# Two neighbouring blocks' outputs in one buffer and one 1 MB store, the last two blocks stored singly

## The chip, the cores and the metric

The kernel runs on one core of a Trainium2 chip. A core has a matrix engine (TensorE, PE), a vector engine (VectorE, DVE), a scalar engine (ScalarE, ACT), GpSimd (POOL) and a sync engine (SyncE, SP), which work side by side and wait for each other by semaphores; data move between the chip's memory (DRAM) and the on-chip buffers by DMA, on 16 DMA engines. The metric is the device time of one execution in microseconds; lower is better.

## The reference

The input is four images of 256 channels by 64 by 64 pixels in f32. Layer 0 normalises each image in 32 groups and adds a 3 by 3 neighbourhood attention to the input. Layer 1 takes the pixels as tokens, adds a gated windowed mean over 64 tokens, and then a mixture of eight experts of which each token uses two. Cut to the part that the changed stage completes:

```python
def _from_tokens(t, like):
    B_, C_, H_, W_ = like.shape
    return t.transpose(0, 2, 1).reshape(B_, C_, H_, W_)

x = x + _L0_conv_ref(_gn(x), ...)
t = _to_tokens(x)
t = t + _L1_attn_ref(_ln_t(t), ...)
t = t + _L1_ffn_ref(_ln_t(t), ...)     # out = tokens + combine[:, e:e+1] * y for each expert e
x = _from_tokens(t, x)
```

## The kernel before

The kernel handles the image in NB = 32 blocks of BT = 512 pixels (eight rows of 64), eight blocks (IB) to an image. It has three loops, one after the other. The token loop makes the tokens and scatters each to its two experts. The expert loop runs 71 tiles of 512 tokens through the experts' two layers and scatters the answers, two for each token, into the DRAM tensor `answers`. The output loop, which this case is about, takes for each block the two answers of each of its 512 tokens, adds them, turns them from tokens to channels, and stores them to `out_x`.

The output loop is laid over four engines, each with its own queue of instructions in program order, all unrolled:

- SP (`output_loop_sync`, L1913) loads 1 MB of `answers` per block into one of GOT = 4 buffers `got`. From the fifth block on it waits first until the sum of the block four earlier is made. A partition's share of such a load is 8 KB that lie together in DRAM.
- DVE (`output_loop_vector`, L1926) waits for the load, and until PE has turned the block two earlier, and adds the two answers into one of two buffers `tot`.
- PE (`output_loop_tensor`, L1938) turns the block by eight 128 by 128 transposes into two PSUM banks (`m_bank`, two pairs used in turn), for which it waits until ACT has emptied them two blocks earlier.
- ACT (`output_loop_scalar`, L1952 and L1956) copies the two banks, 128 by 512 each, into one of FIN = 3 buffers `fin`, and issues the store of 512 KB itself. Ahead of the copies it waits until the store that last used the buffer has landed (`fin_out`), and ahead of the store until its own two copies are written (`f_taken`).

So the load of block n waits for the sum of n-4, that for the transposes of n-6, those for the copies of n-8, and those for the landing of the store of n-11. A channel's pixels lie together in DRAM, so a store of one block consists of 256 pieces (128 partitions, two halves `c` of the channels) of 512 pixels, 2 KB each, and neighbouring blocks of an image lie next to each other in each channel. Loads go by the SP queue (q1 in the profile) and stores by the ACT queue (q10), both to the same 16 DMA engines.

Of the kernel before, what the change touches and what calls it, by code (L numbers as in the profile page):

```python
# [88 lines left out]
def hybrid(nc, x, wqT, wkT, wvT, wo, bq, bk, bv, bo, wpT, bp, wg, rwT, w1, b1, w2, b2, out):  # L89
# [6 lines left out]
    ACT = mybir.ActivationFunctionType  # L96
    AX = mybir.AxisListType

    P = 128
    NI, C, H, W = x.shape  # L100
    CC = C // P
# [3 lines left out]
    BT = ROWS * W  # L105
    KT = BT // P
    IB = H // ROWS
    NB = NI * IB
# [17 lines left out]
    ov = out.rearrange("i (c p) h w -> p c i (h w)", p=P)  # L126

    ctx = ExitStack()
    with ctx:
# [3 lines left out]
        def sem(name):  # L133
            return ctx.enter_context(nc.semaphore(name))

        def sig(name, order):
            return Signal(sem(name), order)
# [214 lines left out]
        def enter(eng, part):  # L352
            eng.wait_ge(left[part], 5)
# [1295 lines left out]
        def tiles_loop(eng, n, body, first=-3):  # L1649
            for off in range(first, n + 2):  # L1650
                body(Iteration(None, off, n))
# [237 lines left out]
        def cb(name, shape, dt=f32):  # L1889
            return loop3.enter_context(nc.sbuf_tensor(name, shape, dt))  # L1890

        GOT, FIN = 4, 3
        got = cb("got", [P, GOT, KT, 2, C])
        tot = cb("tot", [P, 2, KT, C])
        fin = cb("fin", [P, FIN, CC, BT])
        tot_ready = sig("tot_ready", "Kt")
        f_full = [sig(f"f_full{i}", f"Kf{i}") for i in range(2)]
        f_taken = [sig(f"f_taken{i}", f"Kk{i}") for i in range(2)]
        got_in = [sem(f"got_in{i}") for i in range(GOT)]
        fin_out = [sem(f"fin_out{i}") for i in range(FIN)]  # L1900

        def turned_bank(it, c):
            return m_bank[it.parity("K") * CC + c]
# [38 lines left out]

        def output_loop_scalar(eng):
            enter(eng, 2)
            def body(it):
                if it.runs("K"):
                    blk = it.block("K")
                    if blk >= FIN:
                        eng.wait_ge(fin_out[blk % FIN], blk // FIN * 16)
                    for c in range(CC):  # L1950
                        f_full[c].wait(eng, it, f"Kf{c}")
                        eng.activation(fin[:, blk % FIN, c, :], turned_bank(it, c)[:, :], ACT.Copy).then_inc(f_taken[c].sem, 1)  # L1952
                    for i in range(CC):
                        f_taken[i].wait(eng, it, f"Kk{i}")
                    dst = ov[:, :, bass.ds(blk // IB, 1), bass.ds(blk % IB * BT, BT)]
                    eng.dma_start(dst, fin[:, blk % FIN, :, :]).then_inc(fin_out[blk % FIN], 16)  # L1956
            tiles_loop(eng, NB, body)
            for i in range(FIN):
                eng.wait_ge(fin_out[i], 16 * ((NB - i + FIN - 1) // FIN))
        loop3.close()  # L1960
        last_blocks.close()

        with nc.Block() as block:
# [20 lines left out]
            @block.scalar  # L1984
            def _(eng):
                prologue_scalar(eng)
                token_loop_scalar(eng)
                expert_loop_scalar(eng)
                output_loop_scalar(eng)
# [42 lines left out]
```

## Time and profile before

| | us |
|---|---|
| median of 3 runs | 1447.72 |
| lowest and highest of them | 1446.48, 1451.52 |
| the profiled execution's own time | 1442.31 |
| its span, first to last instruction | 1440.5 |
| the output loop in it, from the first load's start to the end | about 129 |

The profile shows one execution. Its page gives each engine's busy time and a picture of the span in 40 slices; behind it the trace answers for any stretch: busy time by engine, the share of the 16 DMA engines that packets took (1.00 is all of them all the time; slightly more can come out, since neighbouring packets overlap), the bytes moved by each queue, the instructions in order of time, and which wait ended last. Times in such answers count from the start of the span.

### The profile page before, as it was taken

What the parts mean: (1) busy time and instruction counts of PE and PEld (TensorE: products, weight loads), DVE (VectorE), ACT (ScalarE), POOL (GpSimd) and SP (SyncE); (2) the same over time, 40 slices, a digit from 0 to 9 for tenths busy, and PEclk for the clock granted to TensorE, in tenths of its full rate; (3) what the DMA queues carried; (4) which work ended last, traced back from release to release, by engine and by line L of the source; (5) the groups of instructions that cost most, each with busy time, mean ns of one, the idle gap of its engine ahead of it and who ended that gap; (6) DMA issues with size and microseconds to landing.
All of it is one profiled execution on the core that took longest, in us unless ns stands there. A gap on an engine that the chain in (4) does not pass through costs nothing. (4 is left out here: it accounts for less than half of the span.)

```text
span 1440.5 us, 28874 instructions
## 1 busy us (share of the span) xinstructions
PE 1285.4 (89%) x8512; PEld 1130.3 (78%) x8512; DVE 1127.6 (78%) x3903; ACT 987.1 (69%) x2090; POOL 746.9 (52%) x963
## 2 busy tenths in 40 slices
PE   3799999999999999999999589999999999993434
PEld 3688888888888888888887478899999999982334
DVE  5478888888888777878786778899999999983323
ACT  1677777777777777777775468888888888871223
POOL 2115656566656566566655465566566656662000
PEclk9999999999999999999999679999999999996555
DMA  8622535363542122222111189988888888856999
GB/s 273 216 83 80 149 86 148 88 156 89 147 117 91 58 83 64 82 69 86 50 42 57 36 277 326 300 270 270 277 271 270 273 263 275 279 194 273 416 400 350
DMA packets 148216, 264.00 MB, mean 183 GB/s; under 512 B 52576, under 2 KB 74720, under 8 KB 143840
## 3 DMA queue, kind: packets, MB, share of 16 engines
q1 hardware_dynamic: 113440, 173.78, 38.6%
q0 software_dynamic: 25920, 71.60, 14.0%
q10 hardware_dynamic: 8704, 16.78, 3.0%
q8 instruction: 73, 1.20, 0.4%
q14 instruction: 79, 0.65, 0.2%
HBM read 128.39 MB, written 100.68 MB: 159 GB/s over the span
## 5 line engine op out<-in xcount | busy, mean ns | idle before, releaser
L1716 POOL DMA_INDIRECT answers<-yy,dest_i x284 | 276.7, 974 | 176.7 <-DVE yy L1837 99.7
L1558 POOL DMA_INDIRECT sent<-tn,slot_s x256 | 275.5, 1076 | 146.7 <-issue 79.2
L1768 PE MATMUL s_bank<-band,hh 128*128 x568 | 163.2, 287 | 0.6 <-DVE yy L1872 0.6
L1768 PE MATMUL s_bank<-w_s,hh 128*128 x568 | 157.2, 277 | 0.0
L1768 PE MATMUL s_bank<-band,hl 128*128 x568 | 157.0, 276 | 0.0
L1802 ACT ACTIVATE hid<-m_bank,b1s 128x512 f32<-128x512 f32 x142 | 97.7, 688 | 78.3 <-PE m_bank L1751 50.3
L1822 ACT ACTIVATE zz<-xin 128x256 f32<-128x256 f32 x284 | 147.5, 602 | 0.0
L758 PE MATMUL m_bank<-wvo,band 128*128 128x258 f32 x792 | 132.7, 304 | 13.3 <-DVE band L1390 10.9
L1535 POOL TENSOR_TENSOR rs<-ve,halves 128x4 f32<-128x4 f32 x64 | 64.9, 1019 | 153.7 <-DVE ve L1252 153.7
L790 PE MATMUL o_bank<-vv,at 128*128 128x256 f32 x512 | 138.7, 393 | 1.3 <-DVE tt L1300 0.8
L758 PEld LDWEIGHTS m_bank<-wvo,band 128*128 128x128 f32 x792 | 107.1, 192 | 29.4 <-issue 27.7
L1938 PE MATMUL m_bank<-ident,tot 128*128 128x128 f32 x256 | 54.6, 391 | 80.7 <-ACT fin L1952 58.6
L1837 DVE SCALAR_TENSOR_TENSOR yy<-yy,pick,zz 128x256 f32<-128x256 f32 x284 | 118.7, 480 | 7.4
L758 PE MATMUL s_bank<-band,rT 128*128 128x256 f32 x768 | 123.1, 296 | 0.0
L1751 PE MATMUL m_bank<-xh,w1hs 128*128 128x512 f32 x284 | 112.5, 396 | 4.5 <-DMA b2s<-in_b 4.5
L1938 PEld LDWEIGHTS m_bank<-ident,tot 128*128 128x128 f32 x256 | 46.1, 207 | 89.1 <-issue 66.6
L1751 PE MATMUL m_bank<-xh,w1ls 128*128 128x512 f32 x284 | 112.4, 396 | 0.0
L1751 PE MATMUL m_bank<-xl,w1hs 128*128 128x512 f32 x284 | 112.1, 395 | 0.0
L1926 DVE TENSOR_TENSOR tot<-got 128x1024 f32<-128x1024 f32 x32 | 39.1, 1225 | 92.6 <-PE m_bank L1938 64.9
L1952 ACT ACTIVATE fin<-m_bank 128x512 f32<-128x512 f32 x64 | 34.9, 595 | 107.6 <-DMA out_x<-fin 77.1
L1768 PEld LDWEIGHTS s_bank<-band,hh 128*128 128x128 f32 x568 | 106.8, 188 | 0.9 <-issue 0.8
L1768 PEld LDWEIGHTS s_bank<-w_s,hh 128*128 128x128 f32 x568 | 106.9, 188 | 0.1
(238 smaller groups left out, 3658.9 us busy)
## 6 DMA issues: line engine op xcount, KB each, us to landing
xin<-sent SPq DMA_DIRECT2D x71, 524.0 KB, 4.7
got<-answers SPq DMA_DIRECT2D x32, 1024.0 KB, 9.7
w1hs<-rT SPq DMA_DIRECT2D x71, 256.0 KB
w1ls<-w_s SPq DMA_DIRECT2D x71, 256.0 KB
xs<-in_x SPq DMA_DIRECT2D x32, 512.0 KB, 5.0
raw<-in_x SPq DMA_DIRECT2D x32, 512.0 KB
out_x<-fin ACTq DMA_DIRECT2D x32, 512.0 KB, 10.0
b2s<-in_b SPq DMA_DIRECT2D x71, 128.0 KB
```

The source lines that it names most:

```text
L758: last = eng.matmul(dst, lhs(i, c), rhs(j, c), start=(n == 0), stop=(n == len(passes) - 1))
L790: last = eng.matmul(o_bank[:, 0:C], at[:, k % 2, j, :], vv[:, value_slot(it.block("B"), k + j), 0:C], start=(j == 0), stop=(j == 1))
L1535: eng.tensor_tensor(rs[:, n, :], ve[:, n, :], halves[:, 0, 0:KT], ALU.pow).then_inc(root.sem, 1)
L1558: eng.indirect_dma_start(sent, bass.IndirectOffsetOnAxis(slot_s[:, par, j, k:k + 1], 0), tn[:, par, k, :], None).then_inc(scattered[par], 16)
L1716: eng.indirect_dma_start(answers, bass.IndirectOffsetOnAxis(dest_i[:, at_ % RING, k:k + 1], 0), yy[:, slot, k, :], None).then_inc(rows_out ...
L1751: last = eng.matmul(h_bank[f][:, :], w[:, at_ % WS, c, fs], xx[:, par, c, :], start=(n == 0), stop=(n == 3 * CC - 1))
L1768: last = eng.matmul(y_bank[half][:, k * C:(k + 1) * C], hx[:, par, f, ts], rhs, start=(n == 0), stop=(n == 3 * CC - 1))
L1802: eng.activation(hid[:, f, :], h_bank[f][:, :], ACT.Gelu, bias=b1s[:, at_ % WS, f:f + 1])\
L1822: last = eng.activation(zz[:, at_ % WS, k, :], row[:, 0:C], ACT.Identity, bias=row[:, C + 5:C + 6], scale=row[:, C + 4:C + 5])
L1837: last = eng.scalar_tensor_tensor(row, row, pick[:, at_ % RING, k:k + 1], zz[:, at_ % WS, k, :], ALU.mult, ALU.add)
L1926: eng.tensor_tensor(tot[:, it.parity("K"), :, :], got[:, blk % GOT, :, 0, :], got[:, blk % GOT, :, 1, :], ALU.add).then_inc(tot_ready.sem, 1)
L1938: last = eng.transpose(turned_bank(it, c)[:, k * P:(k + 1) * P], tot[:, it.parity("K"), k, c * P:(c + 1) * P], ident[:, :])
```

## The change

A `fin` buffer becomes twice as wide and holds two neighbouring blocks, an even one and the odd one behind it. ACT waits for a free buffer only ahead of the even block, copies four banks into it, and issues one store of 1 MB behind the odd block, in which each piece is 1024 pixels, 4 KB. The last two blocks (30 and 31) have a buffer and a 512 KB store each. There are still three buffers, and the other engines' instructions are untouched.

```diff
--- before.py
+++ after.py
@@ -1892,7 +1892,7 @@
         GOT, FIN = 4, 3
         got = cb("got", [P, GOT, KT, 2, C])
         tot = cb("tot", [P, 2, KT, C])
-        fin = cb("fin", [P, FIN, CC, BT])
+        fin = cb("fin", [P, FIN, CC, 2 * BT])
         tot_ready = sig("tot_ready", "Kt")
         f_full = [sig(f"f_full{i}", f"Kf{i}") for i in range(2)]
         f_taken = [sig(f"f_taken{i}", f"Kk{i}") for i in range(2)]
@@ -1942,21 +1942,32 @@
 
         def output_loop_scalar(eng):
             enter(eng, 2)
+            ALONE = NB - 2
+
+            def stored(blk):
+                return blk // 2 if blk < ALONE else ALONE // 2 + blk - ALONE
+
             def body(it):
                 if it.runs("K"):
                     blk = it.block("K")
-                    if blk >= FIN:
-                        eng.wait_ge(fin_out[blk % FIN], blk // FIN * 16)
+                    n = stored(blk)
+                    half = blk % 2 if blk < ALONE else 0
+                    if n >= FIN and half == 0:
+                        eng.wait_ge(fin_out[n % FIN], n // FIN * 16)
                     for c in range(CC):
                         f_full[c].wait(eng, it, f"Kf{c}")
-                        eng.activation(fin[:, blk % FIN, c, :], turned_bank(it, c)[:, :], ACT.Copy).then_inc(f_taken[c].sem, 1)
-                    for i in range(CC):
-                        f_taken[i].wait(eng, it, f"Kk{i}")
-                    dst = ov[:, :, bass.ds(blk // IB, 1), bass.ds(blk % IB * BT, BT)]
-                    eng.dma_start(dst, fin[:, blk % FIN, :, :]).then_inc(fin_out[blk % FIN], 16)
+                        eng.activation(fin[:, n % FIN, c, half * BT:(half + 1) * BT], turned_bank(it, c)[:, :],
+                                       ACT.Copy).then_inc(f_taken[c].sem, 1)
+                    if blk >= ALONE or half == 1:
+                        for i in range(CC):
+                            f_taken[i].wait(eng, it, f"Kk{i}")
+                        first, size = (blk, BT) if blk >= ALONE else (blk - 1, 2 * BT)
+                        dst = ov[:, :, bass.ds(first // IB, 1), bass.ds(first % IB * BT, size)]
+                        eng.dma_start(dst, fin[:, n % FIN, :, 0:size]).then_inc(fin_out[n % FIN], 16)
             tiles_loop(eng, NB, body)
+            last = stored(NB - 1) + 1
             for i in range(FIN):
-                eng.wait_ge(fin_out[i], 16 * ((NB - i + FIN - 1) // FIN))
+                eng.wait_ge(fin_out[i], 16 * ((last - i + FIN - 1) // FIN))
         loop3.close()
         last_blocks.close()
 
```

On ACT, where the output loop begins (`hid` and `hh` are the last two copies of the expert loop), before:

```order
L1802 ACTIVATE hid<-m_bank,b1s 128x512 x2
L1813 ACTIVATE hh<-hid 128x512 x2
L1952 ACTIVATE fin<-m_bank 128x512 x2
L1956 DMA out_x<-fin 128x2x512
L1952 ACTIVATE fin<-m_bank 128x512 x2
L1956 DMA out_x<-fin 128x2x512
```

and of the change:

```order
L1802 ACTIVATE hid<-m_bank,b1s 128x512 x2
L1813 ACTIVATE hh<-hid 128x512 x2
L1959 ACTIVATE fin<-m_bank 128x512 x4
L1966 DMA out_x<-fin 128x2x1024
L1959 ACTIVATE fin<-m_bank 128x512 x4
L1966 DMA out_x<-fin 128x2x1024
```

The first block's store has moved behind the second block's copies, and so for each of the first fifteen pairs; the 64 copies are the same in number and size, the 32 stores are 17.

On ACT, at the end of the program, of the change (before, the pattern of two copies and one store of 512 goes on to the end):

```order
L1959 ACTIVATE fin<-m_bank 128x512 x4
L1966 DMA out_x<-fin 128x2x1024
L1959 ACTIVATE fin<-m_bank 128x512 x2
L1966 DMA out_x<-fin 128x2x512
L1959 ACTIVATE fin<-m_bank 128x512 x2
L1966 DMA out_x<-fin 128x2x512
```

The end is as it was: the last two blocks go out one by one, behind the pair of blocks 28 and 29.

## Rows read from the trace of the kernel before

**Rows 1.** The page: engines' busy time; DMA's busy tenths in 40 slices.

```profile
PE 1285.4 (89%) x8512; PEld 1130.3 (78%) x8512; DVE 1127.6 (78%) x3903; ACT 987.1 (69%) x2090; POOL 746.9 (52%) x963
...
DMA  8622535363542122222111189988888888856999
```

**Rows 2.** The chain that ended last: shares of the span; its first piece here.

```profile
by line: DMA out_x<-fin 6.3%; ACT fin L1952 1.2%; DMA got<-answers 0.7%; ACTq L1956 0.2%; DMA answers<-yy,dest_i 0.2%; issue 0.2%; DVE tot L1926 0.1%; SPq L1913 0.1%; PE m_bank L1938 0.0%; ACTq L80 0.0%; POOLq L350 0.0%
...
1311.73 9.64 DMA got<-answers
```

**Rows 3.** The output loop in stretches: length, engines' busy us, PEclk, DMA share, GB/s.

```profile
1311.50:1325.00 13.50, 4.70 (x24) 3.85 (x24) 4.79 (x4) 3.42 (x6) 0.00 (x0) 0.63 0.98 388
1325.00:1355.00 30.00, 11.69 (x48) 9.40 (x48) 8.69 (x8) 4.82 (x9) 0.00 (x0) 0.50 1.02 421
1355.00:1384.00 29.00, 13.68 (x64) 11.78 (x64) 9.71 (x8) 8.40 (x17) 0.00 (x0) 0.59 1.03 412
1384.00:1391.00 7.00, 4.35 (x24) 3.85 (x24) 3.67 (x3) 3.06 (x6) 0.00 (x0) 0.76 0.95 334
1391.00:1407.00 16.00, 5.44 (x26) 4.80 (x27) 2.77 (x3) 4.19 (x8) 0.00 (x0) 0.57 1.02 414
1407.00:1414.00 7.00, 4.41 (x24) 3.77 (x22) 3.35 (x3) 2.33 (x5) 0.00 (x0) 0.68 0.95 326
1414.00:1428.00 14.00, 4.22 (x18) 3.13 (x16) 3.29 (x3) 2.29 (x5) 0.00 (x0) 0.50 1.02 418
1428.00:1440.50 12.50, 6.15 (x32) 5.57 (x32) 2.83 (x3) 6.39 (x12) 0.00 (x0) 0.64 0.74 280
```

**Rows 4.** DMA queues, 1311.5 to 1440.5 us: packets, MB, share of 16 engines.

```profile
q1 hardware_dynamic: 4608, 33.56, 64.4%
q10 hardware_dynamic: 8704, 16.78, 33.9%
```

**Rows 5.** DMA queues, 1325 to 1350 us; last, the stores' queue from 1320 to 1325.

```profile
q1 hardware_dynamic: 1148, 8.36, 79.2%
q10 hardware_dynamic: 1146, 2.22, 22.9%
...
q10 hardware_dynamic: 34, 0.07, 3.6%
```

**Rows 6.** What concerns `fin`: ACT's idle time by releaser; the stores' landing.

```profile
  DMA out_x<-fin: 77.1, 22
...
DMA to landing us min/median/max: 2.7/10.0/18.6
```

**Rows 7.** DVE in order of time: start us, us, what, idle before and its releaser.

```profile
1321.40 1.23 DVE L1926 TENSOR_TENSOR tot<-got 128x1024 f32<-128x1024 f32 x1 [1.95 <-DMA got<-answers]
...
1374.96 1.22 DVE L1926 TENSOR_TENSOR tot<-got 128x1024 f32<-128x1024 f32 x1 [4.71 <-PE m_bank L1938]
1381.20 1.22 DVE L1926 TENSOR_TENSOR tot<-got 128x1024 f32<-128x1024 f32 x1 [5.02 <-PE m_bank L1938]
```

**Rows 8.** DMA queue of the loads, 1384 to 1390 us and 1408 to 1414 us.

```profile
q1 hardware_dynamic: 227, 1.73, 85.6%
...
q1 hardware_dynamic: 184, 1.40, 71.3%
```

**Rows 9.** ACT in order of time: start us, us, what.

```profile
1320.19 0.42 ACTq L1956 DMA_DIRECT2D out_x<-fin  x1
...
1324.54 0.38 ACTq L1956 DMA_DIRECT2D out_x<-fin  x1
...
1430.70 0.38 ACTq L1956 DMA_DIRECT2D out_x<-fin  x1
...
1432.35 0.38 ACTq L1956 DMA_DIRECT2D out_x<-fin  x1
...
1437.30 0.38 ACTq L1956 DMA_DIRECT2D out_x<-fin  x1
```

**Rows 10.** DMA queue of the expert loop's scatters, 1000 to 1100 us.

```profile
q0 software_dynamic: 3013, 8.21, 20.7%
```

## The prediction

> **What bounds the kernel now.** I read the page first: TensorE is busy for 89% of the span, but the last three of the 40 slices show DMA at nine tenths [rows 1]. These are the output loop, and the diff touches nothing else, so what the change is worth is decided in the last 129 us. Then the chain of waits: out of those 129 us, 6.3% of the span, 91 us, are stores of `fin` in flight [rows 2]. That alone would mislead: a store "in flight" may be waiting its turn among the loads. So I read the stretches with their DMA share. From 1325 to 1384, 1391 to 1407 and 1414 to 1428 us the 16 engines are at 1.02 to 1.03, at 412 to 421 GB/s; only the start (0.98), two stretches of 7 us (0.95, at 334 and 326 GB/s) and the last 12.5 us (0.74) fall short [rows 3]. No compute engine is near its limit there. The loop is bound by the DMA engines' packets; the waits of ACT matter only where they leave those engines short of packets.
>
> **The price of the packets.** From 1325 to 1350 us both queues are always full. Loads took 79.2% of 25 us for 8.36 MB, 2.37 us per MB; stores took 22.9% for 2.22 MB, 2.58 us per MB [rows 5]. At these prices all 33.56 MB of loads cost 79.5 us and all 16.78 MB of stores 43.3 us [rows 4], together 122.8 us out of the loop's 129.0. What is over lies, by the bytes of each stretch at these prices, in three places [rows 3]. Start: 5.24 MB in 13.5 us, 12.4 us of loads, 1.1 us over. The two slow stretches: 2.34 and 2.28 MB, some 2.4 us per MB, 1.4 and 1.5 us over. End: 3.5 MB in 12.5 us, 9.0 us of stores, 3.5 us over. The sum, 7.5 us, is 1.3 more than the difference, 6.2, as the other stretches run at a share over 1.00.
>
> **Why the slow stretches exist.** The same 25 us show how the engines share themselves: 1148 packets of loads against 1146 of stores [rows 5], one for one, whatever their size. A load packet is 8 KB (8.36 MB make 1020; the others are small completion packets), a store packet 2 KB, so stores get a fifth of the bytes where a third is needed. A load of a block then moves in 128/16 = 8 turns, a store in 16, so loads run at twice the stores' pace in blocks. ACT falls behind and waits 77.1 us in 22 waits for a landing; half the stores take over 10.0 us to land, one 18.6 [rows 6]. By the chain of buffers DVE stands too: its sums at 1374.96 and 1381.20 us are 6.2 us apart, both released by PE, which waited for ACT [rows 7]. Each sum lets SP issue one load, and a load takes about half that to move, so the load queue runs dry, and when it starts again its packets are slow: 85.6% of 6 us for 1.73 MB is 2.97 us per MB, 71.3% for 1.40 MB is 3.06 [rows 8], against 2.37. The two slow stretches are such restarts; why the packets are slow in them the trace doesn't say.
>
> **The change part by part.**
>
> Packets of 4 KB in place of 2 KB. Fifteen pairs carry 15.73 MB of the 16.78. If a packet costs a fixed part and a part by size, 2 KB at 2.58 and 8 KB at 2.37 us per MB (rates from [rows 5]) differ by 0.21 us for 488 - 122 = 366 packets per MB, which is 9 ns of one engine for each; 4 KB are 244 packets fewer than 2 KB, so 2.58 - 0.14 = 2.44. The expert loop's scatters also write DRAM: 20.7 us for 8.21 MB is 2.52; in 3013 packets there is room for 2004 of 4 KB, and the other 1009 at 9 ns are 0.6 us, which leaves 2.45 [rows 10]. I take 2.44: 15.73 MB by 0.14 saves 2.2 us, with the completion packets of 15 stores fewer 2.3. Bounds: nothing, and 15.73 by 0.21, 3.3 us. The Trainium skill gives 512 B as the least transfer for line rate (DMA: Bandwidth & Descriptors, Specifications). By that rule 2 KB is at line rate and this term is 0, the sum 3.0; the trace disagrees by the 0.21 us per MB between the queues, though part of that may be the direction.
>
> The share between the queues. One for one with 4 KB against 8 KB, stores get the third of the bytes that they need: a 1 MB store is again 16 turns, and so are the two loads that belong to it. A turn is 8 KB by 2.37 and 4 KB by 2.44 us per MB times 16 engines, 0.31 + 0.16 = 0.47 us, so 7.5 us for a pair in both queues. ACT's need is 2.9 us in that time (next but one paragraph), so it should hardly wait, SP should keep three or four loads queued, and the restarts should go. Of their 2.9 us I take 2.0 as gained, since something may still upset the balance (instruction fetches, a late pair); bounds 0 and 2.9.
>
> The later first store. It moves from 1320.19 behind the second block's copies, some 1.7 us later. Loads alone fill the engines up to there (share 0.98), and even with 512 KB in hand the store queue is not what is short; nothing, and at most the 1.1 us of the start more. Three buffers now hold six blocks, so a load is chained to a landing 13 or 14 blocks back and not 11; that only gives slack.
>
> The end. Now ACT sets the pace behind the last load: from one store's issue to the next 1.65 us, 0.38 of it the issue [rows 9], while the packets of 512 KB need 0.524 by 2.58 = 1.35 us. For a pair ACT needs 3.3 less one issue, 2.9 us, its packets 1.05 by 2.44 = 2.56. More important is the backlog. Loads begin at 1311.7 [rows 2] and move alone until about 1324 us (34 store packets by 1325, where a full us has 46 [rows 5]), 1.1 us of it lost: 11.3 us by 2.48 us a block (1.05 MB by 2.37), 4.6 blocks ahead. Both then move at 3.75 us a block, so loads end at 1324 + 27.4 by 3.75 = 1426.8 us with 4.6 blocks still to store, 5.9 us of packets, to 1432.7. The last block's store can be issued 3.1 us after its load is seen (1321.40 to 1324.54 for an unhindered block [rows 7, 9]) and its packets start within about 1.3 us (landing takes 2.7 us at least [rows 6], 1.35 of it packets): near 1431.2, just before only its own 1.35 us of packets are left. So the engines stay nearly full. What must remain of the 3.5 us is 1.35 us of landing and the 0.5 us between the last landing (1437.30 + 2.7 = 1440.0) and the end of the span [rows 6, 9]; I leave 0.7 us for ACT's pace, a gain of 1.0 us. Bounds: a loss of 1.0, if the chain from the last load comes 2 us later than that, and a gain of 1.6.
>
> ACT's own 15 issues fewer (0.38 us each) lie under DMA time except at the end, where they are counted.
>
> Sum: 2.3 + 2.0 + 1.0 = 5.3 us; bounds -2.1 and 7.8 taken all together. The profiled execution took 1442.31 us, span 1440.5; by the sum it would be 1437.0 and 1435.2. The median of the runs is 5.4 us above the profiled one; I take the same 5.3 us off it: 1442.4 us, 0.37% less.
>
> **The rivals.** (a) Partial: 4 KB packets are no cheaper, since the difference between the queues is one of reading and writing DRAM, or restarts come anyway, as the pieces are coarser. For it: no 4 KB packet of this queue is in the trace, and the two stretches are too few to be sure of their cause. Against: the scatters' 2.45. With half the restarts' gain and the end's, 1.0 + 1.0, it gives 1445.7 us.
> (b) Each store pays for its landing. A store takes 2.7 us at least for 1.35 us of packets, and 15 fewer would save 15 by 1.35, 20 us: 1427.5. The skill's fit of 2.0 us fixed plus bytes by 436e3 per us (DMA: Bandwidth & Descriptors, Anatomy of one DMA) speaks for something like it. Against: at shares of 1.02 other packets fill those gaps.
> (c) Slower. A buffer comes free only as a whole MB, so ACT may stand longer at a time, and the four `got` buffers run dry at each reuse; every restart costs about 1.45 us. There are 14 reuses; if all are restarts, 20.3 us less the 2.9 there are, less 3.3 from the other terms, is 14 us more: 1461.8. It decides from about seven restarts on (5 more by 1.45 against 3.3 and 4.3). For it: 22 waits now, landings of up to 18.6 us, which get longer with size; "Splitting DMAs into smaller chunks may allow some to start sooner", says the Trainium skill (Perfetto Trace Analysis, DMA Optimizations). Against: the one-for-one turns fit 4 KB exactly, and that advice is for idle DMA engines, which the trace shows full.
> (d) Nothing moves because the bytes are the same: every gain above 122.8 us stays lost elsewhere. The same time, 1447.7.
>
> **How the numbers follow.** A measurement of this kernel tells about 0.3%, 4.3 us, from no change. Forecast (4.3 to 7.8 us gained) 0.57; (a), up to 4.3 us, 0.31; (d) 0.05; (b) 0.02; (c) 0.05. Faster 0.59, within 0.3% 0.36, slower 0.05. The likeliest case alone spans 1440 to 1443.4; the range goes on over (a) to 1447.5, and down to 1439.0 for the bound of 7.8 and the scatter of medians.
>
> **What would show it.** In the profile of the changed kernel: q10 with 3840 packets of 4 KB, and in full stretches packet counts still one for one, at 0.16 us per store packet (0.17: no saving); ACT's wait for `out_x` under 25 us in place of 77.1; landings of stores around 8 to 15 us and never 18; no stretch under 380 GB/s between 1325 and 1425 us; the stretch from the last load's end to the last store's packets near 390 GB/s in place of 280. The prediction is wrong if sharing is by bytes or by DMA and not by packets, if the slow load packets come with a full load queue too, or if the stores lag so that ACT still waits.

## The result, and the profile after

The change is faster by about half a per cent. In ten runs of each kernel the ratio of the times is 0.9944 (95% interval 0.9929 to 0.996), some 8 us, where 5.3 were forecast; put on the before time of these runs, 1446.91 us, it gives 1438.8 us, just under the lower end of the range. The medians themselves, 1446.91 and 1441.67 us, lie 5.2 us apart. Timed again later beside the kernel before, the same change gave 0.997 (0.995 to 0.9991), some 4 us. What is sure and what is scatter in this is taken up below.

The output loop of the changed kernel in the same kind of stretches as [rows 3]. The loop begins 2.8 us later in this execution (first load issued at 1313.7 against 1310.9 us), in code that the change doesn't touch. Length, engines' busy us, TensorE's granted clock, DMA share, GB/s:

```profile
1325.00:1355.00 30.00, 16.45 (x71) 13.41 (x72) 10.36 (x9) 9.88 (x18) 0.00 (x0) 0.56 1.01 416
1355.00:1384.00 29.00, 14.34 (x60) 11.15 (x59) 9.81 (x8) 9.25 (x16) 0.00 (x0) 0.50 1.02 425
1384.00:1391.00 7.00, 3.83 (x16) 3.02 (x16) 2.10 (x2) 2.39 (x4) 0.00 (x0) 0.50 1.01 421
1391.00:1407.00 16.00, 8.43 (x35) 6.83 (x36) 5.25 (x5) 4.78 (x8) 0.00 (x0) 0.50 1.02 426
1407.00:1414.00 7.00, 3.39 (x15) 2.58 (x13) 2.45 (x2) 2.39 (x4) 0.00 (x0) 0.50 1.01 424
1414.00:1428.00 14.00, 7.87 (x32) 6.27 (x32) 4.17 (x4) 4.78 (x8) 0.00 (x0) 0.50 1.02 425
1428.00:1438.50 10.50, 3.94 (x16) 3.14 (x16) 1.96 (x2) 2.39 (x4) 0.00 (x0) 0.50 0.67 265
```

The two slow stretches are gone: from 1355 to 1428 us every stretch runs at 421 to 426 GB/s. Who waits for whom in the loop (us in total, times, longest):

```profile
ACT fin L1959 <- PE m_bank L1938: 99.4, 62, 24.0
DVE tot L1926 <- DMA got<-answers: 88.6, 32, 14.1
PE m_bank L1938 <- DVE tot L1926: 70.2, 32, 18.0
```

ACT doesn't wait for a store once; in [rows 6] it was 77.1 us in 22 waits. All 32 sums of DVE now start when a load lands, PE waits for DVE and ACT for PE, so every engine waits in the end for the loads. The queues of the changed kernel from 1350 to 1375 us, against [rows 5], and then over the whole loop from 1311.5 us, against [rows 4] (packets, MB, share of 16 engines):

```profile
q1 hardware_dynamic: 958, 6.93, 65.7%
q10 hardware_dynamic: 957, 3.66, 35.6%
...
q1 hardware_dynamic: 4608, 33.56, 63.4%
q10 hardware_dynamic: 4624, 16.78, 32.4%
```

Turns are one for one again (958 to 957), and since a store packet is now 4 KB, stores get a third of the bytes, 3.66 of 10.59 MB. Over the loop (127 us) stores cost 41.1 us in place of 43.7, loads 80.5 in place of 83.1. The loop, from the first load's issue to the end of the span, is 1438.5 - 1313.7 = 124.8 us against 129.6.

The end, from the timeline of the changed kernel:

```profile
1431.37 1.22 DVE L1926 TENSOR_TENSOR tot<-got 128x1024 f32<-128x1024 f32 x1 [2.63 <-DMA got<-answers]
...
1432.65 1.97 PE L1938 MATMUL m_bank<-ident,tot 128*128 128x128 f32 x8 [1.89 <-DVE tot L1926]
...
1435.34 0.38 ACTq L1966 DMA_DIRECT2D out_x<-fin  x1
```

The last store is issued 3.97 us behind the last load's landing, with TensorE at its lower clock (granted 0.50, 1.2 GHz), and lands at about 1438.0. The loop now ends in this chain and not in ACT's pace: the last 10.5 us run at 265 GB/s, and of these the last 6.5 at 178. The prediction had named near 390 GB/s behind the last load as a sign; that sign failed.

### The profile page after: what moved, and what is told of

The parts are those of the page before. It is cut to its first block and busy times, and to the rows that moved or that the text cites. A ratio compares the mean times of both kernels' runs of the same rounds, so it can differ in the third digit from the quotient of the medians.

```text
span 1438.5 us, 28829 instructions
## 1 busy us (share of the span) xinstructions
PE 1290.5 (90%) x8512; PEld 1130.8 (79%) x8512; DVE 1128.0 (78%) x3903; ACT 991.0 (69%) x2090; POOL 753.0 (52%) x963
## 3 DMA queue, kind: packets, MB, share of 16 engines
q10 hardware_dynamic: 4624, 16.78, 2.9%
## 5 line engine op out<-in xcount | busy, mean ns | idle before, releaser
L1716 POOL DMA_INDIRECT answers<-yy,dest_i x284 | 280.3, 987 | 175.2 <-DVE yy L1837 100.8
L1938 PE MATMUL m_bank<-ident,tot 128*128 128x128 f32 x256 | 62.2, 423 | 70.2 <-DVE tot L1926 70.2
L1938 PEld LDWEIGHTS m_bank<-ident,tot 128*128 128x128 f32 x256 | 49.5, 221 | 82.6 <-DVE tot L1926 64.4
L1959 ACT ACTIVATE fin<-m_bank 128x512 f32<-128x512 f32 x64 | 38.2, 597 | 99.6 <-PE m_bank L1938 99.4
```

Of the source, the lines that this page charges most:

```text
L1716: eng.indirect_dma_start(answers, bass.IndirectOffsetOnAxis(dest_i[:, at_ % RING, k:k + 1], 0), yy[:, slot, k, :], None).then_inc(rows_out ...
L1938: last = eng.transpose(turned_bank(it, c)[:, k * P:(k + 1) * P], tot[:, it.parity("K"), k, c * P:(c + 1) * P], ident[:, :])
```

## The experiments

The theory was that of the prediction, in three terms: cheaper packets (2.3 us), the right share between the queues, so that loads no longer run dry and restart with slow packets (2.0), and a fuller end (1.0). Rivals: that six blocks of buffer are what helps, whatever the packets; and, since 8 us were measured, that the output loop of before is usually worse than in its profile. The kernels ran on four occasions, in which the kernel before took 1562, 1562, 1612 and 1448 us. The difference lies ahead of the output loop: on the second, the kernel before issued its first load of that loop at 1429.8 us and needed 128.2 from there. So lengths of the output loop are compared by the traces, from the first load's issue to the end of the span, and whole times only within one occasion.

**The loop four times over, of before and of the change.** The scatter ahead of the loop is several us; four loops carry the same difference four times.

```diff
+        TB = 4 * NB
...
+                    m = blk % NB
...
-                                  answers[blk * (2 * BT):(blk + 1) * (2 * BT), :].rearrange(
+                                  answers[m * (2 * BT):(m + 1) * (2 * BT), :].rearrange(
```

> The kernel before with its output loop run four times over in one go (128 block steps over the same 32 blocks), so that its losses count four times against the scatter of the loops ahead. Theory 1 (the prediction: the stores' 2 KB packets take turns with 8 KB ones, packets cost 122.8 us a loop, restarts 2.9 us): three loops more cost 3 by 125.7 = 377 us, so about 1824 us. Theory 2 (the profiled execution was a lucky one, the output loop loses some 3 us more on the mean): about 1833 us.

> The change with its output loop run four times over, the last two of the 128 steps stored singly. Theory 1: three loops more cost 3 by 120.5 = 361.5 us, 1442.4 + 361.5 = 1804 us, 20 us below the same with the loop of before. Theory 2: the same 1804 us, since with full queues nothing varies, but 28 us or more below the loop of before.

Measured: 1951.53 and 1907.29 us (medians of five), 44 us apart, twice what theory 1 said. By the traces 1958.8 - 1440.9 = 517.9 us for four loops of before, 129.5 each, and 480.5 for the change, 120.1. The queues of four_before, and then of four_change, over their four loops:

```profile
q1 hardware_dynamic: 18432, 134.23, 66.5%
q10 hardware_dynamic: 34816, 67.12, 33.9%
...
q1 hardware_dynamic: 18432, 134.23, 66.5%
q10 hardware_dynamic: 17680, 67.11, 34.2%
```

The shares read alike, but the first are of 517 us and the second of 479.5: loads cost 2.56 us per MB in the one and 2.37 in the other, the price of full queues. So before, once its loop is under way, loses (2.56 - 2.37) by 33.56 = 6.4 us a loop to slow load packets, against 3.6 in the single pass, which begins with 30 us in which the loads run ahead undisturbed [rows 3]. A long loop gains more by this change than a short one. Theory 1 had 125.7 us for each further loop of before, the rival some 3 more; it was (517.9 - 129.6)/3 = 129.4.

**4 KB pieces for the loads in place of the stores.**

```diff
-                    eng.dma_start(got[:, blk % GOT, :, :, :].rearrange("p k j c -> p (k j c)"),
+                    for h in range(2):
+                        eng.dma_start(got[:, blk % GOT, h * KT // 2:(h + 1) * KT // 2, :, :].rearrange("p k j c -> p (k j c)"),
```

> The kernel before, each 1 MB load issued as two of 512 KB with 4 KB pieces; stores untouched (2 KB pieces). Theory 1 (turns by packet): stores get a third of the bytes, ACT's wait for out_x falls from 77 us to under 15, no slow stretch; but the loads' packets cost 33.56 by 0.07 = 2.4 us more, against 3 us regained: about 0.5 us less than before. Rival (what helps is only that three buffers hold six blocks, or the stores' cheaper packets): ACT's wait stays above 50 us and the time is 2 us or more above before.

Measured: 0.9978 (0.994 to 1.0017), which doesn't tell it from before; the loop is 129.4 us. From 1470 to 1500 us of loads_4k:

```profile
q1 hardware_dynamic: 2233, 8.13, 66.2%
q10 hardware_dynamic: 2234, 4.31, 37.1%
```

One for one with 4 KB against 2 KB: stores get a third of the bytes, 4.31 of 12.44 MB, with their old 2 KB packets. Had engines shared by bytes, or DMA by DMA (a load and a store are 512 KB each here), both would have got the same bytes. ACT's wait fell to 23.6 us in nine waits, not quite under 15. The same lines give prices: 2.44 us per MB for 4 KB loads (66.2% of 30 us for 8.13 MB), what was forecast for 4 KB stores, and still 2.58 for 2 KB stores, so it is the size and not the direction that makes a packet dear. The loads' dearer packets take the gain back, as forecast, and so do two stretches that were not: the first 15.3 us run at 329 GB/s and the last 9.1 at 190. The share alone is not worth anything if it is bought by smaller packets on the larger stream.

**Six buffers of one block.**

```diff
-        GOT, FIN = 4, 3
+        GOT, FIN = 4, 6
```

> The kernel before with six fin buffers of one block (the memory of the change) and its single stores of 2 KB pieces. Theory 1: stores still get a fifth of the bytes, so the backlog grows to six blocks and ACT still waits, over 40 us; some restarts go, the end keeps a backlog: 1 to 2 us less than before. Rival (buffers are what counts): ACT's wait nearly gone, the full 5 us less.

Measured: 0.999 (0.995 to 1.0031), which with that occasion's scatter tells little; the loop is 1545.4 - 1421.1 = 124.3 us, 5.3 less than before and no more than the change's. What concerns `fin` in this kernel, as in [rows 6]:

```profile
  DMA out_x<-fin: 60.8, 19
...
DMA to landing us min/median/max: 4.7/21.4/32.6
```

ACT still waits 60.8 us, as theory 1 said and the rival did not, and it costs next to nothing: behind the wait lie up to six stores that keep the engines busy. On the time the rival is right; theory 1 had taken the wait for the loss. The queues of six_buffers from 1470 to 1500 us:

```profile
q1 hardware_dynamic: 1133, 8.26, 65.6%
q10 hardware_dynamic: 2200, 4.24, 36.7%
```

So the stores don't stay at a fifth: over these 30 us they get a third of the bytes, with 2 KB packets. Turns are one for one only while both queues hold work (234 packets to 232 from 1450 to 1455 us). Once ACT's waits hold the loads back through the chain of buffers, the load queue runs short in this kernel too (134 packets to 583 from 1480 to 1485 us) and the stores catch up. What is missing against before is the slow load packets: 65.6% of 30 us for 8.26 MB is 2.38 us per MB, and from 1480 to 1485 us it is 2.37.

**Does that hold once slack is used up? And the other way round, is the share enough with little buffer?** Ahead of that, one more look at before, and the change's buffers without its packets:

```diff
-                        eng.dma_start(dst, fin[:, n % FIN, :, 0:size]).then_inc(fin_out[n % FIN], 16)
+                        for j in ((blk,) if blk >= ALONE else (blk - 1, blk)):
...
+                            eng.dma_start(dst, fin[:, n % FIN, :, at:at + BT]).then_inc(
+                                fin_out[n % FIN], 32 if blk >= ALONE else 16)
```

> The kernel before once more, for its output loop alone, from the first load's issue to the end of the span; 129.6 us in the profile before. If the first profiled execution was a lucky one, this one is 131 us or more, with more slow load packets (q1 above 2.48 us per MB over the loop); if not, 129 to 130.

> The change, but behind each odd block two stores of 512 KB with 2 KB pieces in place of one of 1 MB with 4 KB pieces: the change's buffers and order, without its packets. Theory 1 (turns by packet): the packets' 2.3 us come back, and stores get a fifth of the bytes again: ACT waits for out_x over 40 us; output loop 127 to 129 us. Rival, to which six_buffers gave 124.3 us for its loop: six blocks of buffer are enough; its loop is 124 to 125 us in one pass as well.

The loop of before took 128.2 us here, so its first profile was no lucky one. pair_two_stores took 1551.7 - 1427.0 = 124.7 us, ratio 0.9987 (0.9951 to 1.0023): the rival's number, not theory 1's 127 to 129, with ACT waiting 68.8 us. The ratios of single loops on these occasions can't tell 5 us from nothing, so this rests on the loops of one trace each. Then four loops, with `FIN` = 6 single buffers, and with the change's wide buffers but `FIN` = 2:

> Four output loops in one go with six buffers of one block and 2 KB pieces. Theory 1: six blocks of slack carry one loop of 32 blocks but not 128; once they are used up the loads run dry as before: 126 us a loop or more, slow load packets as in four_before, ACT waiting for out_x over 200 us. Rival (buffers alone): 120.1 + 2.3 = 122.4 us a loop, since only the packets' price is missing.

> Four output loops of the change with two buffers of two blocks in place of three, so four blocks of buffer and 4 KB pieces. Theory 1 (the share by turns is what counts): with the stores' share right, little buffer is needed; a 1 MB store lands 11 to 15 us after its issue where a pair comes every 7.5, so two buffers are just short and ACT waits some: 120 to 123 us a loop, shares above 1.00. Rival (six blocks of slack are what counts): 126 us a loop or more.

The loops are 1916.3 - 1428.5 = 487.8 us, 121.9 a loop, and 1922.8 - 1442.0 = 480.8, 120.2 a loop. Both remedies hold by themselves (one execution each). Six blocks of slack keep the engines full through 128 blocks with 2 KB packets, against my expectation of 126 or more, though ACT waits 308.4 us, and are dearer than the change by 1.8 us a loop, about the packets' 2.3. With 4 KB packets four blocks of buffer do as well as six (120.2 against 120.1), though ACT waits 272.1 us in 63 waits. The kernel before lacks both: three blocks of buffer are too few for stores in 2 KB packets beside loads in 8 KB packets.

**Four separate passes.** Each pass waits until the stores of the one ahead have landed, so each has the loop's own start and end:

```diff
+                    if m == 0 and blk > 0:
+                        landed(eng, blk)
```

> The kernel before with its output loop run four times over, and each pass starting only when the stores of the one ahead have landed: four samples of the loop as the kernel has it, start and end included, in each execution. If the two single profiles (129.6 and 128.2 us) are typical: 4 passes of 129, three of them added to the kernel before. If the first profile was lucky: 131 to 133 us a pass.

> The same four separate passes of the change's output loop. Theory 1: 124 to 125 us a pass (124.8 in the single profile), every pass alike within 0.5 us since nothing runs dry; 4 by 4.8 = 19 us below passes_before. Theory 2 (the loop of before is typically slower than in its profile and explains the 8 us measured): 32 us below passes_before.

> Four separate passes with six single-block buffers and 2 KB pieces. Buffers-are-enough, as single and joined loops said: 124 to 125 us a pass, though the packets cost 2.3 us more than the change's, because its deeper backlog fills the end.

> Four separate passes of the change in which the first two pairs of a pass go out as two 512 KB stores with 2 KB pieces each, so that the loads get further ahead and the backlog at the end is deeper; all other packets stay 4 KB. If the end of the change is short of stores for want of backlog: 1 to 1.5 us a pass less than passes_change, and the last 10 us of a pass above 300 GB/s. If the end is set by the chain behind the last load alone: the last load comes earlier by the same amount and the gain is the same; no gain at all would mean that the loads do not get ahead.

Medians of six runs, and the four passes of one trace each, from the first load's issue to the end of the span:

| | median, us | span | first load | four passes | a pass |
|---|---|---|---|---|---|
| passes_before | 1997.43 | 1989.1 | 1471.5 | 517.6 | 129.4 |
| passes_change | 1979.13 | 1978.5 | 1481.0 | 497.5 | 124.4 |
| passes_six | 1979.17 | 1967.0 | 1467.2 | 499.8 | 125.0 |
| passes_hybrid | 1967.92 | 1964.2 | 1474.0 | 490.2 | 122.6 |

The first sums of the four passes, of passes_before and then of passes_change:

```profile
1476.92 1.22 DVE L1939 TENSOR_TENSOR tot<-got 128x1024 f32<-128x1024 f32 x1 [14.70 <-DMA got<-answers]
...
1603.27 1.23 DVE L1939 TENSOR_TENSOR tot<-got 128x1024 f32<-128x1024 f32 x1 [11.72 <-DMA got<-answers]
...
1731.92 1.23 DVE L1939 TENSOR_TENSOR tot<-got 128x1024 f32<-128x1024 f32 x1 [12.07 <-DMA got<-answers]
...
1863.21 1.23 DVE L1939 TENSOR_TENSOR tot<-got 128x1024 f32<-128x1024 f32 x1 [12.76 <-DMA got<-answers]
...
1486.34 1.23 DVE L1940 TENSOR_TENSOR tot<-got 128x1024 f32<-128x1024 f32 x1 [13.78 <-DMA got<-answers]
...
1610.34 1.23 DVE L1940 TENSOR_TENSOR tot<-got 128x1024 f32<-128x1024 f32 x1 [10.68 <-DMA got<-answers]
...
1734.64 1.23 DVE L1940 TENSOR_TENSOR tot<-got 128x1024 f32<-128x1024 f32 x1 [10.72 <-DMA got<-answers]
...
1859.04 1.23 DVE L1940 TENSOR_TENSOR tot<-got 128x1024 f32<-128x1024 f32 x1 [10.50 <-DMA got<-answers]
```

Passes of before are 126.4, 128.7 and 131.3 us apart, so one pass of it scatters by some us; those of the change are 124.0, 124.3 and 124.4. The change is worth 5.0 us a pass by the traces, 18.3/4 = 4.6 by the runs: theory 1's 19 us, not the 32 that 8 us in one pass would make. The hybrid, which sends the first two pairs in 2 KB packets, gains 1.8 us a pass more by the traces (11.2/4 = 2.8 by the runs), where 1 to 1.5 were forecast.

**The rest**: the change timed again, the hybrid in one pass, the change's passes with `GOT` = 2, and with all blocks paired (`ALONE` removed).

> The change as it is, timed again beside the kernel before. If its worth is what its output loop shows, 4.7 us, the ratio is near 0.997 and its profiled loop near 124.8 us. If some 3 us more belong to it, the ratio is near 0.995 and the loop of the profile cannot account for it.

> One output loop as in passes_hybrid: the change with the first two pairs as two stores of 512 KB with 2 KB pieces. By passes_hybrid (some 122.5 us a pass): a loop of 122 to 123.5 us, 1.7 us under the change, 6 to 7 us under before.

> Four separate passes of the change with two got buffers in place of four, so that at most two loads are queued and the queue is often empty between them. If load packets are slow wherever a load starts on an empty queue: q1 well above 2.40 us per MB (2.7 or more), DMA share below 1.00 and 150 us a pass or more. If only a deep queue of stores makes them slow: q1 stays at 2.40 and the loss is idle time.

> Four separate passes of the change with the last two blocks as a pair too. The last store can then start only behind both blocks and is twice as long: 1.05 MB by 2.44 less 0.52 by 2.58 = 1.2 us more behind the last load, 125.4 us a pass against 124.2.

change_again: 0.997 (0.995 to 0.9991), loop 1444.1 - 1319.4 = 124.7 us, both as the output loop alone would have it. hybrid: 0.9947 (0.9928 to 0.9965), 1440.76 us against 1443.71 of the change and 1448.32 of before on the same occasion, loop 1440.2 - 1317.5 = 122.7: the fastest version found, 4 KB packets throughout but for the first two pairs. ACT waits 69.7 us for stores in it and not at all in the change, which once more says nothing of the time. Its last 10 us:

```profile
1430.00:1440.00 10.00, 3.64 (x16) 3.27 (x16) 1.16 (x1) 3.65 (x8) 0.00 (x0) 0.50 0.85 342
```

They run at 342 GB/s, against 265 in the last 10.5 of the change. The loads had run further ahead: by 1400 us, 25.70 MB of loads and 8.52 of stores had moved, which in blocks of 1.05 and 0.52 MB is a lead of 8.3 blocks; in the change it was 25.31 and 10.37 MB, 4.4 blocks. The edit against the change, cut:

```diff
+                        if blk < 4:
+                            pieces = [(blk - 1, 0, BT, 16), (blk, BT, BT, 16)]
+                        elif blk >= ALONE:
+                            pieces = [(blk, 0, BT, 32)]
+                        else:
+                            pieces = [(blk - 1, 0, 2 * BT, 32)]
```

passes_all_paired (one execution): 1822.7 - 1320.3 = 502.4 us, 125.6 a pass, 1.2 over the change as forecast, so the two single stores at the end earn their lines. passes_got_two (one execution): 1882.4 - 1318.1 = 564.3 us, 141.1 a pass, slower than the change by 17 us but not the 150 that I expected, with these queues over its four passes:

```profile
q1 hardware_dynamic: 18432, 134.23, 64.8%
q10 hardware_dynamic: 18496, 67.11, 29.2%
```

That is 64.8% of 564.3 us for 134.23 MB of loads, 2.72 us per MB, where passes_change paid 2.40; stores stay at 2.46 (29.2%). In the first pass, from 1330 to 1410 us, the engines are "busy" at 0.96 to 0.98 and move 368 GB/s. The edit made the loads' queue shorter, and the loads' packets got slow.

A short load queue is not enough, though. In six_buffers from 1480 to 1485 us it is as short as in before from 1380 to 1385 (134 load packets to 583 of stores, and 113 to 545), but load packets cost 2.37 us per MB in the one and 2.97 in the other. In before the dear packets go on from 1386 to 1389 us, where no store packet moves at all, while in six_buffers store packets move in every microsecond from 1476 to 1496. So the slow packets seem to need a short queue of stores beside the short queue of loads. No run tests that, and what the engine does in that time none shows.

## Why the prediction was right, and where it was wrong

**What bounds the loop: right.** The time followed packets and their price; ACT's waits, 77.1 us before and none now, 60.8 in six_buffers and 69.7 in the hybrid, say nothing by themselves.

**Packets: right.** Over the separate passes stores cost 2.61 us per MB before (33.8% of 517.6 us for 67.12 MB) and 2.45 after (33.1% of 497.5), 2.6 us a pass for 16.78 MB, forecast 2.3. loads_4k rules out the direction: 4 KB loads cost 2.44. The Trainium skill gives 512 B as the least transfer for line rate (DMA: Bandwidth & Descriptors, Specifications), which would have made this term 0; the 2.61 and 2.45 us per MB of 2 KB and 4 KB packets do not agree with that.

**Share and restarts: the size right, the chain of causes right only in part.** In the separate passes loads fell from 2.46 to 2.40 us per MB (63.9% of 517.6 us and 64.7% of 497.5 for 134.23 MB), 2.2 us a pass, forecast 2.0. Turns are one for one as forecast while both queues are full (958 to 957, and 2233 to 2234 in loads_4k). Two steps failed. I held the share for the only cure, and six buffers of one block do as well but for the packets' price. And the step "the load queue runs dry, and when it starts again its packets are slow" does not hold by itself: in six_buffers the queue runs short too, and its packets cost 2.37 to 2.38 us per MB. My turns also left out the completion packets, 16 to a DMA: two loads take 18 turns and a 1 MB store 17 (4608/32/16 = 9 for a load, 4624/17/16 = 17 for a store), not 16 each, a small slip.

**The end: mis-sized.** The term "a gain of 1.0 us" came to about nothing: 5.0 us a pass less 2.6 and 2.2 leaves 0.2. I had the last load in at 1426.8, 115.9 us after the first load's issue, with 4.6 blocks still to store, and the last store issued 3.1 us behind it. The lead itself came out close: by 1425 us, 32.52 MB of loads and 13.81 MB of stores had moved, 4.7 blocks apart. But the sum by mean rates missed how the last load ends: its last eleven packets took from 1429 to 1431 us while 0.77 MB of stores moved beside them. It was in 117.7 us after the first issue (1431.37 - 1313.7), with 33.56 MB of loads and 15.42 of stores moved, so 2.6 blocks were left and not 4.6. The chain behind it took 3.97 us, since the eight transposes took 1.97 us at the lower clock (granted 0.50), where the row that I read the 3.1 from had them at 1.09 us (granted 0.94). By then the backlog was gone, and the engines stood idle ahead of the last store. The hybrid, which deepens the backlog, takes 1.8 us back.

**The range: wrong at its lower end.** The loop's gain is 4.8 us between the first two traces, 4.2 between the means of both traces of before (129.6, 128.2) and both of the change (124.8, 124.7), 5.0 by the traces of the separate passes and 4.6 by their runs: the forecast of 5.3 is that close. The first timing gave 8 us and the second 4.3, with the same two kernels. By the means it is 1447.4 - 1440.5 = 7.0 us in ten and ten runs whose standard deviations are 3.4 and 2.9 us (1.4 us for the difference), and 1448.3 - 1443.7 = 4.6 (1.3 us) in the second; weighted together, 5.6 with a standard error of 1.0. That agrees with 5 us, but the interval of the first ratio by itself, 5.8 to 10.3 us, does not. That the further 3 us of the first timing are scatter of the loops ahead is the likely reading, not shown run by run: in six profiles at this level of time, with the same code ahead of it, the output loop began at 1310.9, 1313.7, 1319.4, 1317.5, 1318.1 and 1320.3 us. No term of the sum explains them, so their cause stays open. The step that failed is "down to 1439.0 for the bound of 7.8 and the scatter of medians": it left 1 us for that scatter where the runs show 3. How narrow the miss is shows in the time that the ratio is put on: 1446.91 us from ten runs gives 1438.8, the 1447.72 from the three runs that I had gives 1439.6.

**The rivals.** (a) fell: in full stretches a 4 KB packet takes an engine 0.16 us, as a load (2.44 us per MB in loads_4k) and as a store (2.45), and no restart came. (b) fell: fifteen stores fewer would have saved 20 us, and the loop got about 5 shorter; pair_two_stores, with the 32 stores of before, is as short (124.7 us) as the change with 17. The fit of the Trainium skill on which it leaned (DMA: Bandwidth & Descriptors, Anatomy of one DMA) is one for DMAs that GpSimd issues, while ACT issues these. (c) fell: ACT waits at none of the 14 reuses. (d) fell: with the same bytes the loop is shorter, by 4.2 to 5.0 us a pass.

## What to carry to other kernels

When two DMA queues are full at once, compare their packet sizes with the ratio of bytes that the loop needs from each: in these kernels they took turns packet by packet, and the stream with the smaller packets fell behind. Two things cured it here: larger pieces on the stream that falls behind, or enough buffers behind it (six blocks in place of three). Larger pieces also make its packets cheaper, 2.45 us per MB in place of 2.61. Don't let the load queue get short: with at most two loads queued their packets cost 2.72 us per MB, with four 2.40. At the end of such a loop a backlog of stores must cover the chain behind the last load, so the loads should be the ones that run ahead. And an engine's wait says nothing of a loss until you have seen what the bottleneck does during it.

## What was not expected of the hardware

From 1330 to 1410 us of passes_got_two the DMA engines were busy at a share of 0.96 to 0.98 and moved 368 GB/s, in the change at 1.02 they moved 425: most of that difference is in packets that take longer, so the share alone tells that packets are open and not how fast they move. And 30 us at the start of the loop of before hid the steady state: 421 GB/s there, some 390 on the mean of four loops.
